# A decoder layer on one core: first low parts, late norms and late turned weights on other engines, and a new order

## The reference

```python
def _L0_attn_ref(x, Wq, bq, Wk, bk, Wv, bv, Wo, bo, layerscale):
    q, k, v = (einsum('bsd,ed->bse', x, W) + b for W, b in ((Wq, bq), (Wk, bk), (Wv, bv)))
    scores = einsum('bse,bte->bst', _layer_norm(q), _layer_norm(k)) / sqrt(D)
    attn = sigmoid(scores - log(S))
    return (einsum('bsd,ed->bse', attn @ v, Wo) + bo) * layerscale
def _L0_xattn_ref(v, k, q, ...):            # 16 heads of 16, keys and values from ctx
    attn = softmax(qh @ kh.T / sqrt(16)); return merge(attn @ vh) @ dense_w.T + dense_b
def _L0_ffn_ref(x, W_r, W_k, W_v, mu_r, mu_k):
    xr = mu_r * x + (1 - mu_r) * x_prev;  xk = mu_k * x + (1 - mu_k) * x_prev
    r = sigmoid(xr @ W_r.T);  k = xk @ W_k.T
    return r * (square(relu(k)) @ W_v.T)
x = layernorm(x + attn(x)); x = layernorm(x + xattn(ctx, ctx, x)); x = layernorm(x + ffn(x))
```

## Time and profile before

| | |
|---|---|
| median of 3 runs | 555.92 us (555.9 to 558.53) |
| the profiled execution's own time | 557.22 us |
| its span | 555.4 us, so 1.8 us lie around it |
| busy of the span | PE 94%, ACT 83%, DVE 82%, POOL 68% |
| mean granted clock of TensorE | 0.988 of full |

### The profile page before, as it was taken

One profiled execution on the slowest core, in us unless ns is written; L12 is line 12 of the kernel. 1 busy time (PEld: TensorE's weight loads), 2 busy tenths in 40 slices (PEclk: granted clock), 3 DMA queues, 4 the chain that ended last, 5 costly groups with the idle time before them and its releaser, 6 DMA issues.

```text
span 555.4 us, 12598 instructions
## 1 busy us (share of the span) xinstructions
PE 519.7 (94%) x4526; PEld 472.6 (85%) x4526; DVE 454.2 (82%) x987; ACT 460.2 (83%) x1108; POOL 376.9 (68%) x498
## 2 busy tenths in 40 slices
PE   5999998999999999999999999999999678998993
PEld 3887997889989898989898998988889568998982
DVE  4588877878888887979788888777777789999994
ACT  2474469788898988989898989999999889898874
POOL 1666457484868585866667585854756645699996
PEclk9799999999999999999999999999999899999998
DMA  6421200101020102011010101031401000011113
GB/s 175 124 90 28 69 24 0 40 2 39 2 60 1 58 1 60 19 40 41 20 39 1 38 3 39 2 97 39 153 2 39 1 2 0 2 58 40 58 39 114
DMA packets 24400, 23.01 MB, mean 41 GB/s; under 512 B 2346, under 2 KB 24338, under 8 KB 24338
## 3 DMA queue, kind: packets, MB, share of 16 engines
q1 hardware_dynamic: 23634, 21.55, 12.6%
q10 hardware_dynamic: 704, 0.66, 0.5%
HBM read 15.07 MB, written 6.82 MB: 39 GB/s over the span
## 4 chain that ended last, share of the span: by engine, by line
PE 63%; ACT 13%; POOL 12%; DVE 5%; issue 3%; DMA 2%; SPq 0%; POOLq 0%; DVEq 0%; ACTq 0%
PE st L276 14%; PE acc L276 12%; PE proj L276 9%; PE xb L276 9%; ACT p_sb L534 5%; PE xb L1824 5%; POOL y L970 5%; PE xb L1808 5%; PE xb L1795 3%; POOL y L949 3%; ACT L534 2%; POOL rs L958 2%; PE proj L1706 2%; DMA xraw<-in_xT 2%; PE xb L1648 1%
## 5 line engine op out<-in xcount | busy, mean ns | idle before, releaser
L914 POOL TENSOR_TENSOR fold<-p_sb 128x640 f32<-128x640 f32 x32 | 50.1, 1565 | 113.8 <-ACT p_sb L534 113.8
L534 ACT ACTIVATE p_sb<-xb,neg_mx 128x77 f32<-128x77 f32 x512 | 116.6, 367 | 9.8 <-DVE neg_mx L1230 9.6
L919 POOL TENSOR_TENSOR p_sb<-p_sb,rc 128x1280 f32<-128x1280 f32 x32 | 74.9, 2340 | 13.3 <-DVE rc L1243 13.0
L276 PE MATMUL st<-qkT_hi 128*128 128x256 f32 x256 | 76.4, 298 | 0.0
L276 PE MATMUL acc<-vv_hi,aT_hi 128*128 128x256 f32 x256 | 75.3, 294 | 0.0
L276 PE MATMUL st<-qkT_lo,qkT_hi 128*128 128x256 f32 x256 | 72.3, 282 | 0.0
L276 PE MATMUL st<-qkT_hi,qkT_lo 128*128 128x256 f32 x256 | 72.3, 282 | 0.0
L276 PE MATMUL acc<-vv_lo,aT_hi 128*128 128x256 f32 x256 | 72.3, 282 | 0.0
L276 PE MATMUL acc<-vv_hi,aT_lo 128*128 128x256 f32 x256 | 72.3, 282 | 0.0
L1230 DVE TENSOR_REDUCE neg_mx<-xb 128x4 f32<-128x308 f32 x128 | 54.0, 471 | 17.2 <-PE xb L1795 17.0
L1125 DVE TENSOR_TENSOR aT_lo<-a_sb,aT_hi 128x512 fp32r<-128x512 f32 x64 | 55.9, 874 | 2.3 <-ACT aT_hi L444 2.3
(11 more groups left out here) (230 smaller groups left out, 1758.9 us busy)
## 6 DMA issues: line engine op xcount, KB each, us to landing
xraw<-in_xT SPq DMA_DIRECT2D x16, 256.0 KB, 3.4
xs<-in_x SPq DMA_DIRECT2D x16, 256.0 KB, 2.8
out_y<-y SPq DMA_DIRECT2D x16, 256.0 KB, 2.1
x_kept<-xs SPq DMA_DIRECT2D x10, 256.0 KB, 2.2
x2s_a<-x_kept SPq DMA_DIRECT2D x2, 512.0 KB, 4.7
x2s_b<-x_kept SPq DMA_DIRECT2D x2, 512.0 KB, 6.7
x2s_c<-x_kept SPq DMA_DIRECT2D x1, 512.0 KB, 3.7
cT<-in_cT SPq DMA_DIRECT2D x1, 308.0 KB, 3.1
```

Source lines behind the costliest of these rows:

```text
L276: mm = pe.matmul(out, s_, m_, start=first and k == 0 and q == 0, stop=last and k == n - 1 and q == 2, skip_group_check=not check)
L534: ex = act.activation(weights(t)[:, h // KH * (H // 2) + KH * n + h % KH, 0:SC], logits[n][:, h * SC:(h + 1) * SC], ACT.Exp, bias=neg_mx[: ...
L914: pool.tensor_tensor(fold[:].rearrange("p (h k) -> p h k", k=FO), p[:, :, 0:FO], p[:, :, FO:2 * FO], ALU.add).then_inc(fo_pool.sem, 1)
L919: pool.tensor_tensor(weights(t), weights(t), rc[:, t % 2].rearrange("p (h o) -> p h o", o=1) .to_broadcast([P, H, SP]), ALU.mult).then_inc ...
```

## The change

**Engines.** The low parts of x^T of pairs 0 and 1 go from POOL to DVE (`XD = 2`). Both high parts of the q/k weights are now made by ACT. The second norm of pairs 7 to 15 goes from ACT to POOL (`N2 = 7`). Part 2 of the turned weights of tiles 20 to 31 goes from ACT to DVE (`NTA = 20`).

**Loads.** x^T of pair 1 is issued before the q and k biases, x^T of pair 2 (which waits for pair 0's low part) before woT, wv, the scale and bv; woT and the scale move from ACT's queue to SP's; x^T of pair 3 (which waits for pair 1's low part) comes before `bo`. `bo` has a semaphore and a fold of its own.

**Order.** All four lists are written anew; no call is dropped and, apart from those above, none is added. In PE's round scores and attends alternate more, and from `x2(0)` on the last part's products stand earlier among the last cross attention (`x2(0)` ahead of `weights_t(25, 2)` instead of inside tile 27, `receptance(0)` right behind `mixed(13)`).

```diff
@@ constants and who has done it
+XD = 2
+N2 = 7
+NTA = 20
+        def xt_ready(i):
+            return xt_dve.at(i) if i < XD else xt_pool.at(i - XD)
+        def crossed_norm(i):
+            return ln2_act.at(i) if i < N2 else ln2_pool.at(i - N2)
-            return tp_act.at(t) if c == 2 else tp_dve.at(t, c + 1)
+            return tp_dve.at(t, c + 1) if c < 2 else tp_act.at(t) if t < NTA else tpt_dve.at(t - NTA)
@@ sync: first loads
                 load_xt(0)
                 for k in range(KC):
                     sp.dma_start(wraw[:, k, D:2 * D], rows("wkT")[:, k]).then_inc(load_w[k].sem, 16)
+                load_xt(1)
                 sp.dma_start(bqk[:, 0:D], bc("bq")).then_inc(load_b.sem, 16)
                 sp.dma_start(bqk[:, D:2 * D], bc("bk")).then_inc(load_b.sem, 16)
-                load_xt(1)
                 sp.dma_start(ident[:], io["ident"]).then_inc(load_id.sem, 16)
+                load_xt(2)
+                sp.dma_start(wo_ls[:], rows("woT")).then_inc(load1.sem, 16)
                 sp.dma_start(wv_raw[:], rows("wv")).then_inc(load1.sem, 16)
+                sp.dma_start(ls[:], bc("ls")).then_inc(load1.sem, 16)
                 sp.dma_start(bvcol[:], io["bv"]).then_inc(load1.sem, 16)
-                sp.dma_start(bo[:], bc("bo")).then_inc(load1.sem, 16)
-                for i in range(2, 4):
-                    load_xt(i)
+                load_xt(3)
+                sp.dma_start(bo[:], bc("bo")).then_inc(load_bo.sem, 16)
                 load_rows(0)
...
-                w.wait_ge(*wqk_dve.at(0))
+                w.wait_ge(*wqk_dve.at(KC - 1))
                 w.wait_ge(*wvo_pe.at(0))
-                w.wait_ge(*wo_pool.at(0))
+                w.wait_ge(*bo_pool.at(0))
@@ gpsimd
+                def norm2(i):
+                    w.wait_ge(*xds_pool.at(i))
+                    for t in range(2):
+                        x2 = rows_of(i)[:, t]
+                        pool.tensor_scalar(x2, x2, rs2[:, i % 2, t:t + 1], nb2[:, i % 2, t:t + 1],
+                                           ALU.mult, ALU.add).then_inc(ln2_pool.sem, 1)
...
+                    at(norm2, r - 5, NJ, 7)
@@ vector
+                def wqk_lo(k):
+                    w.wait_ge(*wqk_act.at(k))
+                    low_part(w_qk[0][:, k], w_qk[1][:, k], wraw[:, k]).then_inc(wqk_dve.sem, 1)
+                def xt_lo(i):
+                    w.wait_ge(*xt_act.at(i))
+                    low_part(xt_of(i, 0), xt_of(i, 1), xraw[:, i % NXR]).then_inc(xt_dve.sem, 1)
+                def weights_tail(t):
+                    w.wait_ge(*tp_pe.at(t))
+                    w.wait_ge(*pv_pe.at(t // 2 - 1))
+                    dve.tensor_copy(pT[:, 8:NCH, (t % 2) * P:(t % 2 + 1) * P], tiles(tp_bank(2)[:, 0:2 * P])).then_inc(tpt_dve.sem, 1)
...
-                wqk_split()
+                wqk_lo(0)
+                xt_lo(0)
+                wqk_lo(1)
                 qk_bias(0)
                 qk_stats(0)
+                xt_lo(1)
                 qk_bias(1)
@@ gpsimd, written-out part from 431 us on (new order)
+                fold_weights(29)
+                normalise(29)
+                deviation2(12)
+                norm2(11)
+                halo(3)
+                fold_weights(30)
+                norm2(12)
+                normalise(30)
+                fold_weights(31)
+                residual3(0)
+                normalise(31)
+                halo(4)
+                deviation2(13)
+                norm2(13)
@@ tensor: a round of the new order
+                    at(v, r, NJ, 6)
+                    at(scores, 4 * r - 12, NS, 11)
+                    at(dense, r - 7)
+                    at(weights_t, 2 * r - 12, NT, 0, 0)
+                    at(weights_t, 2 * r - 12, NT, 0, 1)
+                    at(tqk, 2 * r, NT, 12)
+                    at(x1, r - 5, NJ, 1)
+                    at(weights_t, 2 * r - 12, NT, 0, 2)
+                    at(attend, 4 * r - 16, NS, 8)
+                    at(qk, 2 * r + 1, NT, 13)
+                    at(query, r - 5, NJ, 1)
+                    at(attend, 4 * r - 15, NS, 8)
+                    at(cross_scores, 2 * r - 10, NT, 1)
+                    at(scores, 4 * r - 11, NS, 11)
+                    at(attend, 4 * r - 14, NS, 8)
...
```

More of the change, by code:

```diff
@@ new lines, in round_ @@
+                    at(exponentials, 2 * r - 5, NT, 2, 0)
+                    at(exponentials, 2 * r - 5, NT, 2, 1)
+                    at(exponentials, 2 * r - 5, NT, 2, 2)
+                    at(exponentials, 2 * r - 5, NT, 2, 3)
+                    at(norm2, r - 6, N2)
+                    at(norm1, r - 2, NJ, 2)
+                    at(sigmoid_hi, 4 * r - 2, NS, 12)
+                    at(tqk_hi, 2 * r + 6, NT, 13)
+                    at(x1_hi, r - 2, NJ, 2)
+                    at(sigmoid, 4 * r - 1, NS, 12)
@@ L1036, in _ @@
                 fold_weights(26)
+                halo(0)
                 residual1(15)
@@ L1081, in _ @@
                 deviation3(4)
-                norm3(3)
+                norm2(14)
+                norm3(4)
                 residual3(5)
-                norm3(4)
+                halo(11)
                 residual3(6)
                 deviation3(5)
-                halo(11)
-                residual3(7)
                 halo(12)
@@ L1110, in _ @@
                     mix_round(i)
-                norm3(10)
-                deviation3(11)
-                residual3(13)
                 deviation3(12)
@@ new lines, in round_ @@
+                    at(crossed, r - 4, NJ, 1)
+                    at(tqk_lo, 2 * r + 6, NT, 15)
+                    at(x1_lo, r - 2, NJ, 3)
+                    at(sums, 2 * r - 5, NT, 4)
+                    at(reciprocals, 2 * r - 5, NT, 4)
+                    at(sigmoid_lo, 4 * r - 2, NS, 15)
+                    at(weights_body, 2 * r - 6, NT, 3, 1)
+                    at(qk_bias, 2 * r + 7, NT, 16)
+                    at(qk_stats, 2 * r + 7, NT, 16)
+                    at(weights_tail, 2 * r - 6, NT, 20)
@@ L1452, in _ @@
                 qk_stats(11)
-                sigmoid_lo(7)
                 maxima(0, 0)
+                maxima(0, 1)
                 qk_norm(11)
-                maxima(0, 1)
+                sigmoid_lo(8)
                 maxima(0, 2)
-                sigmoid_lo(8)
+                tqk_lo(11)
                 maxima(0, 3)
-                tqk_lo(11)
+                qk_bias(12)
+                qk_stats(12)
+                sums(0)
+                reciprocals(0)
+                maxima(1, 0)
@@ L1461, in _ @@
                 attended(1)
+                maxima(1, 1)
                 stats1(1)
-                qk_bias(12)
-                sums(0)
-                qk_stats(12)
-                maxima(1, 0)
-                maxima(1, 1)
-                reciprocals(0)
                 maxima(1, 2)
+                maxima(1, 3)
                 v_bias(6)
-                maxima(1, 3)
                 qk_norm(12)
                 weights_body(0, 0)
+                sigmoid_lo(9)
                 tqk_lo(12)
+                weights_body(0, 1)
@@ new lines, in _ @@
+                maxima(3, 2)
+                stats1(2)
+                maxima(3, 3)
+                v_bias(7)
+                sigmoid_lo(13)
+                qk_norm(14)
+                weights_body(2, 0)
+                sums(3)
+                tqk_lo(14)
+                sigmoid_lo(14)
+                x1_lo(2)
+                weights_body(2, 1)
+                reciprocals(3)
+                crossed(0)
+                qk_bias(15)
+                qk_stats(15)
+                maxima(4, 0)
@@ L1537, in _ @@
                 sums(29)
-                mix_lo(0)
+                crossed(13)
+                key_squares_lo(0)
+                weights_tail(28)
                 reciprocals(29)
-                crossed(13)
-                mixes(1)
+                stats2(13)
                 maxima(30, 0)
@@ L1913, in round_ @@
-                    at(dense, r - 6)
-                    at(tqk, 2 * r + 2, NT, 9)
-                    at(weights_t, 2 * r - 10, NT, 0, 2)
-                    at(x1, r - 4)
-                    at(attend, 4 * r - 12, NS, 2)
-                    at(qk, 2 * r + 3, NT, 10)
-                    at(query, r - 4)
-                    at(attend, 4 * r - 11, NS, 2)
-                    at(cross_scores, 2 * r - 8, NT)
-                    at(attend, 4 * r - 10, NS, 2)
-                    at(attend, 4 * r - 9, NS, 2)
+                    at(scores, 4 * r - 10, NS, 11)
@@ L1925, in mix_round @@
+                    at(cross_scores, 2 * r - 9, NT, 1)
+                    at(scores, 4 * r - 9, NS, 11)
                 def mix_round(i):
-                    at(x2, i - 1, NJ, 30)
-                    at(mix_values, i - 4, NJ, 20)
-                    at(receptance, i - 3, NJ, 14)
-                    at(mix_keys, i - 2, NJ, 49)
+                    at(mix_values, i - 4, NJ, 12)
+                    at(mix_keys, i - 2, NJ, 25)
```

(9 more changed lines are left out.)

766 lines of the change are left out of this document (400 added, 366 removed).

## The result

| | before | after | difference |
|---|---|---|---|
| median of the runs | 556.38 us | 562.61 us | +6.2 |
| profiled execution, own time | 557.22 us | 561.43 us | +4.2 |
| its span | 555.4 us | 559.6 us | +4.2 |

The ratio of the times is 1.0101, with a 95% interval of 1.0069 to 1.0133. The forecast was 549.0 us, in a range of 542.5 to 556.0. It was wrong in sign and by 13.6 us. Executions of one kernel differ that much, in part with the granted clock: of 17 of the kernel before on one chip, four had a mean clock of 0.981, and three of these took 558.1 to 558.2 us (the fourth 555.4), where no other took more than 557.2. What follows splits the 4.2.

What follows compares the result with a forecast made beforehand. PE was taken to bound the full rounds, ACT the late attention, POOL the end. Terms -3.5, -1.5, 0, -5, -2.5, +5.6 sum to -6.9: 550.3 from the profiled 557.22, 549.0 as median; range 542.5 to 556.

Steps and rivals of the forecast that it cites:

- (a): Start: PE's third projection 0.4 to 3.5 us earlier, plus half of the clock's 2.7 us; -3.5 us.
- (b): Filling of the cross attention, 80 to 105 us: part of PE's 3.3 idle us saved; -1.5 us.
- (c): Full rounds, 105 to 342 us: no PE work added, rounds stay at 25.97 us; 0, bounds 0 and +9.
- rival of a wait in each round: Full rounds: the query's copy on ACT comes late, 0.6 us a round over 9 rounds; 554.4 us, chance 0.13.
- (d): Late attention, 342 to 431 us: ACT relieved of 2.0 us a round, rounds fall from 22.4 to 20.9; -5 us.
- the change doesn't do what it says: Late rounds stay at 22.4 us, set by the chain exp, table change, sigmoid, split; 554 us, chance 0.06.
- (e): From 431 to 470 us: reordered calls fill PE's waits; -2.5 us, bounds -6 and +3.
- (f): Last stretch: nearly full POOL gets two more norms of 2.43 us each and a deviation; +5.6 us.
- slower rival: POOL's added norms delay tiles 30 and 31 and the last stretch, and hold DVE; 559.7 us, chance 0.12.

Runs made afterwards that it cites:

- x3: Changed kernel with its late part (from about 340 us) in the order of before, second norms 7 to 15 on GpSimd, tails on ScalarE: 554.93 us, 0.9984 of before.
- d1: Changed kernel plus a tiny Exp ahead of the wait for the row minima, tiles 20 to 31: 554.15 us, 0.9956 of before.
- d4: x4 plus the early Exp ahead of the wait for the minima: 560.05 us, 1.0073 of before.
- f1: d1 with VectorE's low part of softmax block 62 ahead of the half sums of tile 27: 552.90 us, 0.9942 of before.
- x4: Changed kernel with its late part in the order of before, tails 20 to 31 on VectorE and second norms 7 to 15 on GpSimd: 563.82 us, 1.0134 of before.
- x2: Changed kernel with its late part in the order of before, tails 20 to 31 on VectorE, second norms on ScalarE: 563.27 us, 1.0138 of before.
- d0: Changed kernel with its late part in the order and with the owners of before, plus the early Exp for tiles 20 to 31: 554.43 us, 0.9964 of before.
- e3: x3 plus the early Exp: 556.39 us, 0.9992 of before.

## Why the prediction was wrong, by its steps

**(a) and (b), start and filling, -3.5 and -1.5:** right. `qk(8)` came 3.4 us earlier and `cross_scores(2)`, at the end of the filling, 5.6. PE's third projection came at 12.16, inside 10.7 to 13.9, and the waits were those named: the k bias landed 6.5 us after its issue instead of 8.5, DVE went on at 9.78, then the bias, the statistics and the low part:

```profile
9.78 0.69 DVE L1197 TENSOR_TENSOR qk_sb<-xb,bqk 128x512 f32<-128x512 f32 x1 [2.35 <-DMA bqk<-in_bk]
...
12.16 0.47 PE L281 MATMUL xb<-wqk_hi,xT_hi 128*128 128x512 f32 x1 [2.21 <-DVE xT_lo L1170]
```

That is 2.1 us earlier, and the clock gave the rest of the 3.4. (The middle of my 0.4 to 3.5 us is 2.0, not the 2.2 of the sum.) PE's 2.21 us of waiting left the clock at its upper level, 2.4 GHz, where 4.00 us had been followed by the lower.

**(c) The full rounds, 0:** the term measured +0.1 us a round (26.07 against 25.97) and 0.33 in the first, so 1.0 of the 5.6 were gone at `mixed(9)`. The rival of a wait in each round did not come.

**(d) Late attention, -5: this is the step that failed.** It said that "the missing 1.5 us are ACT's" and that ACT's relief would give a round of 20.9. Measured: 23.84, 23.68 and 23.48 us for the three full ones, and 24.78 for the shorter fourth (20.67 before), +8.0 in all. Two errors are in it. The first: a busy share was read as a bound. ACT was full, but in step with the others. With 1.0 us less of it in x3 the round shrank by 0.14, and with the load hidden as well the mean of the first three rounds was still 22.3 (d1, d4). No kernel of the study had a mean under 22.2 there (the shortest single round, in f1, took 21.36). Whether the 1.3 us over my 20.9 are links of the chain or PE's own, the runs don't tell. PE's row should have warned me: it was busy 86.91 of 89, more than ACT. The second error made the sign. The prediction priced the tails' move as two copies of 0.41 us hidden in VectorE's room and counted the table load in ACT's sum. It gave no price to what the move does to ACT's waits: the wait for PE's turns, left out until then, comes back ahead of the exponentials, and the table load falls behind the wait for the minima, on the chain. The rival "the change doesn't do what it says" had the loop of exponential, table change and split, at 0.06, with 0 for (d), and didn't reach the loss either. In the changed kernel's own order the exposed load is 6.2 of the 8.0 us (d1). In the old order it cost 3.2 us from `mixed(9)` to `mixed(13)` (x4 to d4), of which the later start of d4's trace takes back 1.4. Most of the other 1.8 us lies in the fourth step, 22.69 us in d1: VectorE is busy 19.74 us of it, against 16.03 in the kernel before, with the first mixing's products (1.6) and a low part held for 2.76; f1 shows 1.1 us of the step to be that low part.

**(e) 431 to 470, -2.5:** -1.4 between `mixed(13)` and `mixed(15)`. The wait for oT_lo stayed, as said. The new order is better there than this shows: the old order with the moved work needs 49.35 us, the new one 44.32.

**(f) Last stretch, +5.6:** the term was over-sized; +1.1 to the last values and +1.2 behind them, 2.3. x3 has the same 2.3 for the norms alone. I took GpSimd's norm at 2.43 a pair, from the third norm's row. The group of the second norms, behind 436 us, has 0.70 each, 1.4 a pair:

```profile
L972 POOL TENSOR_SCALAR xs<-xs,rs,nb 128x256 f32<-128x256 f32 x10 | 6.9, 696 | 0.1
```

POOL is still nearly full (69.23 of 72.00 in the last window above), and its `y` is still the first line of the chain, though with less than before:

```profile
by line: POOL y L1011 19.2%; issue 10.8%; POOL y L990 10.1%; DVE xm L1340 9.3%; DVE xmT_lo L1170 8.9%; POOL rs L999 6.6%; DVE st L1374 4.1%; PE xb L281 3.8%; DVE kkT_lo L1170 3.7%; DVE y L1364 2.9%; POOL rs L997 2.6%; DVE mv L1381 1.9%; POO
```

The slower rival, at 0.12, had 559.7 us because GpSimd stands in the way. The sign came out so, but not for that reason. x3 speaks against it: the norms cost nothing in the sum. It was right only in that DVE is held by GpSimd, and the lock did come onto the chain, but held by the normalising and not by the norms. Its price of 0.55 us a low part was also misread from the pair at 505.70. The first of the two ran beside the norm and took its usual 0.69. The second ran from 506.31 to 508.08 and ended 0.55 behind POOL's next instruction, the residual:

```profile
506.25 1.28 POOL L949 TENSOR_TENSOR y<-y,x2s_b 128x512 f32<-128x512 f32 x1
```

So the norm held nothing there. The loss came from the tails: with them alone x2 loses 8.8 us. What d1 took away again is the exposed load. What the moved tails cost behind 430 us in the old order (x2, x4, d4) has no cause shown.

## What to carry to other kernels

Before work is moved off an engine, ask which waits stood only with that work and covered others. Here ScalarE's tail had already waited for PE, so its exponentials didn't need to. With the tail gone they had two waits instead of one, and the activation table change of 1.28 us, until then hidden beside the minima, fell behind one of them. A tiny instruction of the next function, issued ahead of the waits, takes the change off the chain: 8.5 us here, and nothing where the load wasn't held (d0, e3). And where an engine is busy 95% of a stretch, check whether another is as full and whether they take turns; then less work on one gives nothing, as the round of x3 did.

## What was not expected of the hardware

The place of the table load was not: with one wait ahead of the exponential it ran 0.6 us before the minima were even begun (x3), with two it stood behind the wait for them. The lock was more exact than I had thought, and more selective: a low part that met a two-input GpSimd instruction of 1.28 to 2.65 us ended 0.54 to 0.56 us after it, and one that met the scale-and-shift of `y` was not held. A scale-and-shift of 128x256 on GpSimd took 0.70 us a piece for `xs` and 1.29 for `y` on average, the same operation and shape in the profile; in the code the first multiplies and adds, the second subtracts and multiplies. I had used the one for the other. Whether the operation makes the difference was not tested.
